# A graph layer with scattered edge rows: half a relu first, an earlier base of ranks, the last mean on ScalarE, a paced TensorE

## What is computed

```python
h = relu(layernorm(x))                                   # 3125 x 64
m = relu(concat(h[dst], edge_attr) @ W1a.T + b1a)        # 53125 x 128, a row per edge
m = m @ W1b.T + b1b
agg = segment_sum(m, src) / maximum(counts(src), 1)      # mean over the edges of a node
z = relu(concat(h, agg) @ W2a.T + b2a) @ W2b.T + b2b
out = x + concat(z, h) @ Wr.T + br
```

## Time and profile before

| | us |
|---|---|
| median of three runs | 594.39 (594.15 to 594.48) |
| the profiled execution, its own time | 594.85 |
| its span, first to last instruction | 593.1 |
| GpSimd busy | 408.2 (69%), 442 instructions |
| TensorE busy (MATMUL) | 383.1 (65%), mean granted clock 0.805 |
| VectorE busy | 318.1 (54%) |
| ScalarE busy | 100.2 (17%) |
| moved by DMA | 116.35 MB |

### The profile page before, as it was taken

The page is one execution under the profiler, slowest core; times in us unless marked ns, Lnnn a source line. Parts: engine busy times, 40 slices in busy tenths (PEclk is TensorE's granted clock), DMA queues, the critical chain, the costliest instruction groups (busy, mean ns, idle before and its releaser), DMA issues.

```text
span 593.1 us, 7898 instructions
## 1 busy us (share of the span) xinstructions
PE 383.1 (65%) x2608; PEld 344.5 (58%) x2608; DVE 318.1 (54%) x1237; ACT 100.2 (17%) x145; POOL 408.2 (69%) x442
## 2 busy tenths in 40 slices
PE   5546947976255267378468551763985928897875
PEld 3445847745145267378457551663875928797754
DVE  6658422334233346357446432562765818888895
ACT  2241511112122021022112220211221211100022
POOL 2677777777777777777777777777777777777000
PEclk9775957678676596788789765968896978999999
DMA  8982845363443695677675647858697594969511
GB/s 195 362 233 88 243 136 170 92 187 101 124 132 125 186 290 182 215 242 228 221 230 161 180 137 234 247 184 255 200 305 235 165 309 126 323 216 315 177 38 57
DMA packets 54637, 116.35 MB, mean 196 GB/s; under 512 B 9869, under 2 KB 30949, under 8 KB 54593
## 3 DMA queue, kind: packets, MB, share of 16 engines
q1 hardware_dynamic: 41281, 85.11, 47.8%
q0 software_dynamic: 13312, 30.70, 16.2%
HBM read 68.62 MB, written 47.14 MB: 195 GB/s over the span
## 4 chain that ended last, share of the span: by engine, by line
POOL 42%; issue 18%; PE 15%; DMA 11%; DVE 7%; SPq 3%; ACT 2%; POOLq 0%; DVEq 0%; ACTq 0%
POOL slots_dram L411 42%; DMA slots_dram<-pay,pos_i 7%; PE bank L912 6%; PE bank L928 5%; DVE oh L523 3%; DMA dstb<-in_dst 2%; DMA rows<-slots_dram 2%; ACT pay L766 1%; PE bank L1001 1%; DVE eo L512 1%; PE bank L876 1%; PE bank L861 1%; SPq L272 1%; PE bank L932 1%; ACT z1T L814 1%
## 5 line engine op out<-in xcount | busy, mean ns | idle before, releaser
L411 POOL DMA_INDIRECT slots_dram<-pay,pos_i x416 | 404.2, 972 | 139.5 <-issue 123.5
L912 PE MATMUL bank<-pw,eo 128*128 128x128 f32 x832 | 142.7, 343 | 166.9 <-DVE eo L512 166.1
L912 PEld LDWEIGHTS bank<-pw,eo 128*128 128x128 f32 x832 | 134.4, 253 | 176.5 <-issue 176.1
L928 PE MATMUL bank<-rows,oh 128*125 128x129 f32 x1050 | 126.0, 275 | 9.8 <-DVE oh L523 9.6
L928 PEld LDWEIGHTS bank<-rows,oh 128*125 128x125 f32 x1050 | 119.7, 188 | 13.7 <-issue 12.9
L766 ACT ACTIVATE pay<-bank 128x1024 f32<-128x1024 f32 x52 | 53.3, 1024 | 409.1 <-PE bank L912 407.9
L523 DVE TENSOR_SCALAR oh<-marks,rows 128x125 f32<-128x125 f32 x525 | 108.1, 293 | 3.1 <-DMA rows<-slots_dram 2.5
L501 DVE COPY pay<-mark 128x8 f32<-128x8 f32 x52 | 10.6, 214 | 142.8 <-DMA slots_dram<-pay,pos_i 142.1
L512 DVE TENSOR_SCALAR eo<-dstb,lane 64x256 f32<-64x256 int32 x208 | 64.0, 367 | 6.0 <-DMA dstb<-in_dst 5.2
L492 DVE TENSOR_TENSOR slot_t<-bank,eq 128x416 f32<-128x416 f32 x26 | 15.3, 590 | 48.7 <-PE bank L876 47.4
L861 PE MATMUL bank<-we_in,hT 65*128 65x128 f32 x208 | 38.5, 347 | 0.7 <-ACT hT L751 0.7
(11 more groups left out here) (138 smaller groups left out, 225.4 us busy)
## 6 DMA issues: line engine op xcount, KB each, us to landing
rows<-slots_dram SPq DMA_DIRECT2D x24, 864.0 KB, 7.5
dstb<-in_dst SPq DMA_DIRECT2D x52, 256.0 KB, 8.5
eo<-in_edges_T SPq DMA_DIRECT2D x52, 256.0 KB, 3.8
rows<-slots_dram SPq DMA_DIRECT2D x12, 720.0 KB, 7.8
slots_dram<-zeros SPq DMA_DIRECT2D x9, 864.0 KB, 7.7
slots_dram<-pay,pos_i POOLq DMA_INDIRECT x416
rows<-slots_dram SPq DMA_DIRECT2D x8, 648.0 KB, 5.5
slots_dram<-zeros SPq DMA_DIRECT2D x3, 1008.0 KB, 7.4
```

The source lines that it names most:

```text
L411: pool.indirect_dma_start(out=slots_dram[:, :], out_offset=bass.IndirectOffsetOnAxis(ap=pos_i[:, u, k:k + 1], axis=0), in_=pay[:, u, k, :] ...
L912: last = T.matmul(bank[:, 2 * (g % 2) + k // 4, (k % 4) * HID:(k % 4 + 1) * HID], eo[:, u, k * 128:(k + 1) * 128], pw[:, g % WB, a, :], st ...
L928: last = T.matmul(o[0:BN, v * SW:(v + 1) * SW], oh2[:, r % 2, n, :], rows[:, sum_no[r] % RR, n, 0:SW], start=(t == 0), stop=(t == C[ph] - ...
```

## The change

Six things change.

1. **Half relu.** For group 0 the relu is cut in two. TensorE signals after the first four tiles (`H_half`), ScalarE makes the relu of these four (`relu_first_group`), and GpSimd waits for that half alone (`rl_half`) before its first scatter, and for the other half before the fifth.
2. **Early base.** `ranks_from(0)` goes ahead of the first transposes on TensorE.
3. **A column of ones.** A row of `pay` has a column ONE, set to 1.0 once, behind the mark; the summed width SW goes from 129 to 130, and the count of a node is the sum of this column. `rec_mark`, its iota on GpSimd, its reciprocal and a wait on VectorE are gone.
4. **Mean on ScalarE.** In the tails VectorE makes only the total, the maximum with 1 and the reciprocal. ScalarE makes the mean, one ACTIVATE for each bucket with the reciprocal as its scale, and its loop is put in another order: relu of z for `q-3`, copy of the transposed mean of `q-1`, mean of `q`.
5. **Stores.** The third store of the output becomes two (tails 6, then 7 and 8), and these two are one DMA of 125 rows each in place of 112 and 13.
6. **Pacing.** Each buffer of `pay` has four scatter semaphores in place of one, each counting two tiles. TensorE calls `keep_pace(g)` ahead of each tile of `hidden`, `project_windows` and `sum_round`. For groups 4 to 43 it waits at each quarter of the tiles of the group: at the first for the last quarter of group `g - 4`, then for quarters 0, 1 and 2 of group `g - 3`. Whoever waited for a whole buffer now waits for its four semaphores.

The diff, without the path for malformed inputs and the declarations:

```diff
     SLOTS = sum(C) * NB * 128
-    RW, SW = HID + 16, HID + 1
-    MARK = HID
+    RW, SW = HID + 16, HID + 2
+    MARK, ONE = HID, HID + 1
...
     for ph in range(NPH):
-        m = min(3, TPR // C[ph])
+        m = min(512 // SW, TPR // C[ph])
         for b0 in range(0, NB, m):
...
+    BEHIND, QS = 3, 4
+
+    def tiles_of(g):
+        return max(2 * K, K + (KW if g % 2 == 0 else 0) + sum(matmuls(rounds[r]) for r in after[g]))
+
     def last_touch(r):
...
         def scatters_of(u, g):
-            return 16 * K * len(range(u, g, PB))
+            return 16 * (K // QS) * len(range(u, g, PB))
...
         NJ = len(tails)
-        OUT_AT = [3, 6, NJ]
+        OUT_AT = [3, 6, NJ - 2, NJ]
+        OUT_PARTS = [HALVES, HALVES, [(0, BN)], [(0, BN)]]
...
                     for u in range(PB):
-                        sp.wait_ge(s_sc[u], scatters_of(u, 2 * STARTS[ph + 1]))
+                        for part in range(QS):
+                            sp.wait_ge(s_sc[u][part], scatters_of(u, 2 * STARTS[ph + 1]))
                 if sum_no[r] >= RR:
...
             lo = 0
-            for upto in OUT_AT:
+            for upto, parts in zip(OUT_AT, OUT_PARTS):
                 hi = tails[upto - 1][1] + tails[upto - 1][2]
                 sp.wait_ge(S["oe"], upto)
-                for p0, p1 in HALVES:
+                for p0, p1 in parts:
                     sp.dma_start(o_v[p0:p1, lo:hi, :], ot[p0:p1, lo:hi, :]).then_inc(S["out"], 16)
                 lo = hi
-            sp.wait_ge(S["out"], 16 * len(OUT_AT) * len(HALVES))
+            sp.wait_ge(S["out"], 16 * sum(len(parts) for parts in OUT_PARTS))
             sp.wait_ge(S["flag"], 1)
...
             count(block_no[:], [[1, 2]], 0, 2)
-            count(rec_mark[:], [[0, 1]], 1, 1)
             count(marks[:], [[1, BN]], 1, 0).then_inc(S["const"], 1)
...
                 pool.wait_ge(S["pos"], g + 1)
-                pool.wait_ge(S["rl"], g + 1)
+                if g == 0:
+                    pool.wait_ge(S["rl_half"], 1)
+                else:
+                    pool.wait_ge(S["rl"], g + 1)
                 for k in range(K):
+                    if g == 0 and k == K // 2:
+                        pool.wait_ge(S["rl"], 1)
                     pool.indirect_dma_start(out=slots_dram[:, :], out_offset=bass.IndirectOffsetOnAxis(ap=pos_i[:, u, k:k + 1], axis=0),
-                                            in_=pay[:, u, k, :], in_offset=None, bounds_check=None).then_inc(s_sc[u], 16)
+                                            in_=pay[:, u, k, :], in_offset=None, bounds_check=None).then_inc(s_sc[u][k * QS // K], 16)
...
             V.memset(hT_all[:, PAD_L + N:PAD_L + N + PAD_R], 0.0).then_inc(S["hp"], 1)
-            V.memset(pay[:].rearrange("p u k w -> p (u k) w")[:, :, SW:RW], 0.0).then_inc(S["pad"], 1)
+            V.memset(pay[:].rearrange("p u k w -> p (u k) w")[:, :, SW:RW], 0.0)
+            V.memset(pay[:].rearrange("p u k w -> p (u k) w")[:, :, ONE:SW], 1.0).then_inc(S["pad"], 1)
             center(0)
...
                     if g >= PB:
-                        dve.wait_ge(s_sc[u], scatters_of(u, g))
+                        for part in range(QS):
+                            dve.wait_ge(s_sc[u][part], scatters_of(u, g))
                     V.tensor_copy(pay[:, u, :, MARK], mark[:, g, :])
...
                 for t in range(m * C[ph]):
-                    last = V.tensor_scalar(oh2[:, r % 2, t, :], marks[:], rows[:, sum_no[r] % RR, t, MARK:SW], None, ALU.is_equal)
+                    last = V.tensor_scalar(oh2[:, r % 2, t, :], marks[:], rows[:, sum_no[r] % RR, t, MARK:ONE], None, ALU.is_equal)
                 last.then_inc(S["oh2"], 1)
...
                         limits(ph)
-                    dve.wait_ge(S["const"], 4)
-                    link(V.reciprocal(rec_mark[:], rec_mark[:]))
                 if i == 1:
...
                 dve.wait_ge(S["ag"], r + 1)
+                if q >= 2:
+                    dve.wait_ge(S["sb"], q - 1)
                 V.tensor_tensor(tot[:, q % 2, 0:m, :], sums[:, b0:b0 + m, :], summed(r), ALU.add).then_inc(S["tk"], 1)
                 dve.wait_ge(S["tk"], r + 1)
-                if q >= 2:
-                    dve.wait_ge(S["sT"], q - 1)
                 c = cnt[:, q % 2]
-                link(V.tensor_scalar(c[:, 0:m, 0], tot[:, q % 2, 0:m, MARK], rec_mark[0:BN, :], MAGIC, ALU.mult, ALU.add))
-                link(V.tensor_scalar(c[:, 0:m, 1], c[:, 0:m, 0], -MAGIC, 1.0, ALU.add, ALU.max))
-                link(V.reciprocal(c[:, 0:m, 2], c[:, 0:m, 1]))
-                V.tensor_tensor(sbar[:, q % 2, 0:m, :], tot[:, q % 2, 0:m, 0:HID], c[:, 0:m, 2].unsqueeze(2).to_broadcast((BN, m, HID)),
-                                ALU.mult).then_inc(S["sb"], 1)
+                link(V.tensor_scalar(c[:, 0:m, 0], tot[:, q % 2, 0:m, ONE], 1.0, None, ALU.max))
+                V.reciprocal(c[:, 0:m, 1], c[:, 0:m, 0]).then_inc(S["rec"], 1)
...
                 if g >= PB:
-                    act.wait_ge(s_sc[u], scatters_of(u, g))
+                    for part in range(QS):
+                        act.wait_ge(s_sc[u][part], scatters_of(u, g))
                 A.activation(pay[:, u, :, 0:HID], bank[:, b:b + 2, :].rearrange("p b (k h) -> p (b k) h", h=HID), ACT.Relu).then_inc(S["rl"], 1)
+
+            def relu_first_group():
+                act.wait_ge(S["H_half"], 1)
+                A.activation(pay[:, 0, 0:K // 2, 0:HID], bank[:, 0, :].rearrange("p (k h) -> p k h", h=HID), ACT.Relu).then_inc(S["rl_half"], 1)
+                act.wait_ge(S["H"], 1)
+                A.activation(pay[:, 0, K // 2:K, 0:HID], bank[:, 1, :].rearrange("p (k h) -> p k h", h=HID), ACT.Relu).then_inc(S["rl"], 1)
...
             copy_window(1)
-            relu(0)
+            relu_first_group()
             relu(1)
...
-            for q in range(NJ + 2):
+            def mean(q):
+                r, b0, m = tails[q]
+                act.wait_ge(S["rec"], q + 1)
+                if q >= 2:
+                    act.wait_ge(S["sT"], q - 1)
+                for v in range(m):
+                    last = A.activation(sbar[:, q % 2, v, :], tot[:, q % 2, v, 0:HID], ACT.Copy, scale=cnt[:, q % 2, v, 1:2])
+                last.then_inc(S["sb"], 1)
+
+            def mean_T(q):
+                r, b0, m = tails[q]
+                act.wait_ge(S["sT"], q + 1)
+                if q >= 2:
+                    act.wait_ge(S["z"], q - 1)
+                A.copy(sbarT[:, q % 2, 0:m * BN], bank[:, 7, 0:m * BN]).then_inc(S["sTe"], 1)
+
+            def relu_z(q):
+                r, b0, m = tails[q]
+                act.wait_ge(S["za"], q + 1)
+                if q >= 2:
+                    act.wait_ge(S["o"], q - 1)
+                A.activation(z1T[:, q % 2, 0:m * BN], zt[:, q % 2, 0:m * BN], ACT.Relu).then_inc(S["zr"], 1)
+
+            for q in range(NJ + 3):
+                if 3 <= q:
+                    relu_z(q - 3)
+                if 1 <= q <= NJ:
+                    mean_T(q - 1)
                 if q < NJ:
-                    r, b0, m = tails[q]
-                    act.wait_ge(S["sT"], q + 1)
-                    if q >= 2:
-                        act.wait_ge(S["z"], q - 1)
-                    A.copy(sbarT[:, q % 2, 0:m * BN], bank[:, 7, 0:m * BN]).then_inc(S["sTe"], 1)
-                if q >= 2:
-                    r, b0, m = tails[q - 2]
-                    act.wait_ge(S["za"], q - 1)
-                    if q >= 4:
-                        act.wait_ge(S["o"], q - 3)
-                    A.activation(z1T[:, q % 2, 0:m * BN], zt[:, q % 2, 0:m * BN], ACT.Relu).then_inc(S["zr"], 1)
+                    mean(q)
...
                 for c in range(KW):
+                    if i >= 2:
+                        keep_pace(2 * i - 2)
                     n0 = PAD_L + window(i, c)
...
-            transpose_h(0)
-            pe.wait_ge(s_w[0], 16)
-            pe.wait_ge(S["ones"], 3)
-            project_windows(0)
-
             def ranks_from(ph):
...
                 T.matmul(RANK, ones_row[:], base[:, ph, :].unsqueeze(1).to_broadcast((1, PK, NQ)), start=True, stop=True, skip_group_check=True)
+
+            pe.wait_ge(S["ones"], 3)
+            pe.wait_ge(S["const"], 3)
+            ranks_from(0)
+            transpose_h(0)
+            pe.wait_ge(s_w[0], 16)
+            project_windows(0)
...
+            paced = [0]
+
+            def keep_pace(g):
+                tile, paced[0] = paced[0], paced[0] + 1
+                if BEHIND < g < STEADY_UNTIL:
+                    for part in range(QS):
+                        if tile == -(-part * tiles_of(g) // QS):
+                            v, q = divmod((g - BEHIND) * QS + part - 1, QS)
+                            pe.wait_ge(s_sc[v % PB][q], scatters_of(v % PB, v + 1))
+
             def hidden(g):
+                paced[0] = 0
                 u = g % EB
...
                     a = k // (K // KW)
+                    keep_pace(g)
                     if k % (K // KW) == 0:
...
```

(14 more changed lines are left out.)

11 lines of the change are left out of this document (5 added, 6 removed).

## The result

The changed kernel takes 592.15 us in the median of 15 runs, the kernel before 595.49 beside it; the ratio of the changed kernel to the kernel before is 0.9941 (95% interval 0.9923 to 0.996), a gain of 3.5 us (3.3 by the medians) where 5.7 were forecast. The time lies above the range of 586.0 to 591.2.

What follows compares the result with a forecast made beforehand. GpSimd's never-resting scatters were taken as the bound, between a head and tails run in a row. -2.8 (head) + 0 (pacing) + 0.4 (waits, sums) - 4.0 (tails) + 0.7 (stores) = -5.7 from 594.39 gave 588.7 us, range 586.0 to 591.2.

Steps and rivals of the forecast that it cites:

- The term for the stores: Last output stores: 125-row DMAs on few engines outweigh the saved issue, +0.7 us, bounds -0.4 and +1.5.
- Rival C: Last output stores: the 125 rows run on five engines at the mean packet, 589.5 us; chance 0.17.
- The first scatter: Head: early base and half relu let GpSimd's first scatter start 3.8 us earlier, at 14.1.
- what of this is kept: Head to group 4: the relu there, behind a dst load, limits the gain to -2.8 us, bounds 3.8 and 2.0 kept.
- the 33rd scatter: First scatter of group 4: waits on that group's relu and starts near 57.6, where it stood at 60.43.
- Rival A: Head: group 4's relu also moves or comes just in time, so 3.8 us stay, 587.7; chance 0.17.
- The tails: Tails: VectorE's work shrinks and steps fall from about 3.04 to 2.6-2.7 us; -4.0 us, bounds -2.5 and -4.8.
- Rival B: Tails: another chain binds, the step falls only to 2.9, -2.5 in place of -4.0, 590.2 us; chance 0.15.
- The pacing: Pairs of groups: TensorE's pacing waits fall within idle time it has anyway; 0 us.
- Rival D: Pairs of groups: pacing makes TensorE wait inside odd groups, slower at 601 us; chance 0.03.
- More waits and wider sums: VectorE, ScalarE, SyncE waits mostly hidden until 485.74, plus sums of 130 columns: +0.4 us, bounds 0 and +1.0.
- The sum: Whole kernel: all terms together give -5.7 us, from the median 594.39 to 588.7.

Runs made afterwards that it cites:

- e4: The kernel before with only the new stores (third store in two, each one DMA of 125 rows): 736.36 us, ratio 0.9971.
- e1: The changed kernel with its last two stores cut into 112 and 13 rows again: 731.99 us, ratio 0.9933 to the kernel before.
- e9: The kernel before with twelve more semaphores that nothing sets or waits for: ratio 0.9995.
- e10: The kernel before with three waits on long-set semaphores wherever the change waits for four in place of one: ratio 1.0013.
- e13: The kernel before with twelve more semaphores, each set once by GpSimd behind the last scatter, none waited for: ratio 0.999.
- e17: The kernel before with twelve 256-byte transfers on SyncE's queue, each signalling its own semaphore, waited for ahead of the stores: one execution, end 5.05 us.
- e18: The kernel before with twelve 256-byte transfers issued by GpSimd behind its last scatter, each signalling its own semaphore: one execution, end 5.19 us.
- e14: The changed kernel without pacing, with two semaphores a buffer and the dst load of group 3 issued early: 589.0 us, ratio 0.9867 to the kernel before.
- e6: The changed kernel without pacing and with one semaphore a buffer: 729.06 us, ratio 0.9904 to the kernel before.
- e12: The changed kernel itself measured again, on the chip of e11: 591.81 us, ratio 0.996 to the kernel before.
- e16: The kernel before with four semaphores a buffer and the waits on them, nothing else: 598.82 us, ratio 1.004.
- e11: The changed kernel without pacing, with one semaphore a buffer and the dst load of group 3 issued early: 587.3 us, ratio 0.9885 to the kernel before.
- e15: The changed kernel without pacing, with four semaphores a buffer and the dst load of group 3 issued early: 591.17 us, ratio 0.9915 to the kernel before.
- e2: The changed kernel with keep_pace never waiting, four semaphores a buffer kept: 731.05 us, ratio 0.9922 to the kernel before.

## Why the prediction was wrong

**The end, the step that failed.** The term for the stores, +0.7 between the last store's issue and the end, was put there for the 125 rows. It measured +3.1 in the first profile (7.9 against 4.8) and +2.7 between the means. The mechanism was wrong: the 125-row stores do take few engines (a share of 0.30 to 0.32 of the 16 in e4), though the last of them moves for 1.75 there and not for the 2.7 that the mean packet gave for five, and they cost nothing that shows (5.1 with them in e4, 7.95 with them cut in e1). What grew the end are the four semaphores a buffer: every kernel with them ends 7.9 to 8.0 after its last addition, every kernel with one 4.9 to 5.5, the one with two 6.6, whatever else it has. I had costed these semaphores only by their waits on the engines, and not looked at what a program does when its last instruction of work is through. Rival C (589.5, the sum with the upper bound of +1.5 for the stores) had the right term and the wrong cause.

Why they do it stays open. It is not their bare number, not their being set by an engine or by a separate DMA, and not the count of waits (e9, e10, e13, e17, e18). Untried is what is left: semaphores that the scatters themselves signal in turn, and waits on those, all through the program. In every kernel a last fetch of instructions, a packet of q8, starts 2.7 to 4.2 us after the last packet of the stores. With four semaphores that is 2.3 to 2.9 ahead of the end of the span, with two (e14) 0.9 ahead of it, and with one 0.3 to 0.9 behind it: it is the end that moves against the fetch. That the fetch has to do with the cause was not shown, and traffic that stops early is no mark of it by itself: in e6, with one semaphore and an end of 5.27, the last packet inside the span (of q14) also stands 2.7 us ahead of the end.

**The head, mis-sized by its starting point.** The first scatter came at 13.85 to 13.95, forecast 14.1. The term "what of this is kept" was -2.8 with 2.0 as its lower bound; it measured -1.94 between the first two profiles, and -1.6 between the means. The wait was as forecast (on the relu of group 4, by way of the `dst` load), and so was the 33rd scatter: near 57.6 forecast, 58.49 and 57.19 measured, 57.8 in the mean. What was off is where it had stood. The 60.43 was one profile's; in the other kernels without the new head the 33rd starts at 58.8 to 59.7, so less was there to be gained. That the `dst` load does not move was right in e12 (it lands at 34.32; at 34.0 to 35.0 in the kernel before, e9, e10 and e16), and not in the first profile (35.56). With the load early (e11, e14, e15) the head keeps 59.4 - 56.2 = 3.2, most of the 3.8. Rival A, the full 3.8 without that, is refuted by the wait.

**The tails, right in the sum and partly by luck.** -4.0 was forecast, and -3.8 came in the first profile. But there TensorE's clock had fallen; where it does not fall the term is -5.1, beyond its bound of -4.8, and the parts of the sum do not fit: from the fourth sum to the ninth 3.8 in e12 (2.5 forecast), ahead of the fourth 0.8 (1.4), behind the ninth 0.55 (0.1). A step is 2.27 to 2.44, below my 2.6 to 2.7. I had added 0.80 for z1 and 0.70 for outs from the steps before; without the wait between them the next group starts after 0.63 and 0.60. VectorE, for which I had 2.3, has no wait either, so which of the two sets the step was not told apart. Three small ACTIVATEs take 0.99, not 0.8, and are hidden as I said. No run shows the 0.3 for one more hand-over from VectorE to ScalarE: in the changed kernel ScalarE starts a mean 0.03 to 0.04 after the reciprocal that it waits for has ended (573.95 after 573.92, 576.39 after 576.35). Rival B (a step of 2.9) is refuted.

**The pacing, right.** 0 was the term. TensorE never waits for a scatter, and its waits for the one-hots are 166.0 with it and 166.1 before. The whole time is less sharp: e15 against e12 gives 0.9915 against 0.996, 2.7 us, of which the 33rd scatter explains 1.2; the rest is within the intervals. Rival D (601) is refuted.

**More waits and wider sums, not told.** +0.4 was the term; the stretch of scatters in the first profile was 2.55 longer than in before's, which a single pair of profiles would have made a finding. Over the ten runs of the table it is 487.1 to 490.0 with both kinds mixed.

**The sum.** What was found is -1.6 - 4.5 + 2.7 = -3.4, for -5.7. With the end at 2.7 and the head at 1.9 the forecast would have been 591.6. The starting point did the rest: the kernel before took 594.39 in the three runs that the forecast started from, and 595.49 beside the changed one. So 1.1 of the 3.45 between 588.7 and 592.15 is not in any term, and without it the time would have been just inside the range, with the same step wrong.

## What to carry to other kernels

Cost a change in the bookkeeping (more semaphores for a finer wait) at the end of the program too, by the time from the last useful instruction to the end of the span; here the four semaphores took back over half of what the tails gained (2.7 of 4.5), for a pacing that was never seen to wait. A gain at the head goes as far as the next load that does not move with it (here 4.05 us were won at the first scatter and 1.94 kept at the 33rd, 3.2 with the load early): look which it is and issue it earlier in the same edit. And take a milestone (the 33rd scatter, the stretch between two scatters) from several profiles before you forecast from it or explain a microsecond of it.

## What I had not expected of the hardware

- The last stretch of the program depends on how many semaphores the scatters signal: 4.9 to 5.5, 6.6 and 7.9 to 8.0 us for one, two and four a buffer.
- The same kernel takes 594 to 597 us on some chips and 730 to 735 on others. The scatters are as long on both; in e2, 96.9 us of TensorE's idle time ahead of its tiles have no releaser (0.7 in the changed kernel), and GpSimd waits 129 us for relus. The cause is open.
- TensorE's granted clock fell to 0.56 in the mean of 3.7 us in the first tails, in one execution and not in another of the same kernel (1.00). The tails take 24.01 in the three profiles with the fall and 22.7 in the six without, 1.28 us less.
